# Gated slot attention with a feed-forward layer: both states from one product with e^s stationary, and the low-rank products of two chunks at once

## The reference

```
q, k = rope(x Wq^T), rope(x Wk^T);  v, g = x Wv^T, x Wg^T
s  = clip(x Ws1^T Ws2^T + bs2, -32, 32)        # low rank: 16
z  = cumlogsumexp(s, over rows);  es = exp(s);  enz = exp(-z)
ok = enz * (tril(q k^T / sqrt(128)) es);  qv = softmax(ok, over the 64 slots)
o  = tril((qv * enz) es^T) v
o  = o * rsqrt(mean(o^2) + 1e-5) * g_norm * (g * sigmoid(g))
x1 = layernorm(x + o Wo^T);  out = layernorm(x1 + x1 (W * scale)^T + bias)
```

## Time and profile before

| | us |
|---|---|
| median of 3 runs | 1460.3 (1459.96 to 1460.4) |
| the profiled execution | 1457.91 |
| its span | 1456.1 |
| busy: PE, PEld | 1426.3, 1204.2 |
| busy: DVE, POOL, ACT | 951.5, 521.1, 491.3 |
| mean granted TensorE clock | 0.996 of full |

### The profile page before, as it was taken

How to read it: one execution, slowest core, us unless ns; L and a number is a source line. 1 busy time by engine, 2 the same in 40 slices (tenths; PEclk the granted TensorE clock), 3 DMA queues, 4 the chain that set the end, 5 groups by cost and what they waited for, 6 DMA issues and landing times.

```text
span 1456.1 us, 23764 instructions
## 1 busy us (share of the span) xinstructions
PE 1426.3 (98%) x9664; PEld 1204.2 (83%) x9664; DVE 951.5 (65%) x1635; ACT 491.3 (34%) x965; POOL 521.1 (36%) x440
## 2 busy tenths in 40 slices
PE   5999999999999999999999999999999999999988
PEld 4888888888888888888888888888888888888876
DVE  5756666566765666567765656657675666657677
ACT  4323223233322323223432322223432222323356
POOL 3322333334433333234533323334432333333255
PEclk9999999999999999999999999999999999999999
DMA  5210111113211201112211110222222021201223
GB/s 203 81 36 33 66 44 59 37 64 120 75 69 44 72 23 55 62 57 97 102 66 30 54 64 26 70 73 67 87 80 66 24 72 44 69 26 66 66 99 118
DMA packets 39562, 97.06 MB, mean 67 GB/s; under 512 B 4384, under 2 KB 4512, under 8 KB 35616
## 3 DMA queue, kind: packets, MB, share of 16 engines
q1 hardware_dynamic: 36864, 90.85, 18.7%
q10 hardware_dynamic: 2592, 4.72, 0.9%
HBM read 74.58 MB, written 20.97 MB: 66 GB/s over the span
## 4 chain that ended last, share of the span: by engine, by line
PE 85%; POOL 7%; DVE 3%; issue 2%; ACT 2%; DMA 0%; POOLq 0%; SPq 0%; ACTq 0%; DVEq 0%
PE bank_kg L941 25%; PE bank_qv L941 13%; PE bank_a L941 12%; PE bank_t L973 6%; POOL o_gated L463 5%; PE bank_wo L1183 4%; PE bank_e L986 3%; PE bank_wo L1159 3%; POOL rms L461 2%; PE bank_a L999 2%; PE bank_qv L958 2%; PE bank_qv L960 2%; PE bank_qv L961 2%; PE bank_c L1188 2%; DVE sum_sq L907 2%
## 5 line engine op out<-in xcount | busy, mean ns | idle before, releaser
L461 POOL TENSOR_TENSOR rms<-var,minus_half 128x4 f32<-128x4 f32 x64 | 65.1, 1017 | 537.3 <-DVE var L910 537.3
L941 PE MATMUL bank_kg<-w_hi,hs_hi 128*128 128x512 f32 x512 | 207.9, 406 | 2.0 <-DVE w_lo L677 1.9
L941 PE MATMUL bank_kg<-w_hi,hs_lo 128*128 128x512 f32 x512 | 202.7, 396 | 0.0
L941 PE MATMUL bank_kg<-w_lo,hs_hi 128*128 128x512 f32 x512 | 201.9, 394 | 0.0
L941 PE MATMUL bank_a<-wo_hi,oT 128*128 128x512 f32 x512 | 174.6, 402 | 0.0
L958 PE MATMUL bank_qv<-hs_hi,w_hi 128*128 128x256 f32 x504 | 146.5, 291 | 9.0 <-DVE w_lo L677 9.0
L758 DVE RECIPROCAL enzT<-cumsT 128x256 f32<-128x256 f32 x64 | 112.2, 1752 | 63.8 <-ACT cumsT L551 51.7
L429 POOL TENSOR_TENSOR k_rot<-rope_a,rope_b 128x512 f32<-128x512 f32 x64 | 82.7, 1292 | 183.4 <-DVE rope_b L706 183.4
L960 PE MATMUL bank_qv<-hs_lo,w_hi 128*128 128x256 f32 x504 | 141.1, 280 | 0.0
L961 PE MATMUL bank_qv<-hs_hi,w_lo 128*128 128x256 f32 x504 | 141.0, 280 | 0.0
L424 POOL TENSOR_TENSOR qT<-rope_a,rope_b 128x512 f32<-128x512 f32 x64 | 82.7, 1292 | 160.7 <-DVE rope_b L718 160.7
(11 more groups left out here) (172 smaller groups left out, 3225.3 us busy)
## 6 DMA issues: line engine op xcount, KB each, us to landing
w_raw<-w_groups SPq DMA_DIRECT2D x28, 1024.0 KB, 5.0
hs_raw<-hs_cols SPq DMA_DIRECT2D x64, 256.0 KB, 2.8
x_scratch<-part SPq DMA_DIRECT2D x64, 256.0 KB, 2.0
part<-x_scratch SPq DMA_DIRECT2D x48, 256.0 KB, 2.8
part<-hs_rows SPq DMA_DIRECT2D x16, 256.0 KB, 3.0
w_raw<-x_scratch SPq DMA_DIRECT2D x16, 256.0 KB, 3.1
w_raw<-w_groups SPq DMA_DIRECT2D x14, 256.0 KB, 6.1
out<-gate ACTq DMA_DIRECT2D x8, 256.0 KB, 2.1
```

The lines of the kernel that those rows point to most:

```text
L461: pool.tensor_tensor(rms[:, :], var[:, :], minus_half[:, :], ALU.pow).then_inc(rms_made, 1)
L941: mm = pe.matmul(dst, x, y, start=start and n == 0, stop=stop and n == 2, **kw)
```

## The change

The rotated k and v of a head stand side by side in one buffer (`kv`). With es of the head as the stationary operand (64 columns), one product of 256 moving columns then makes both es^T k and es^T v, that is, s1 transposed, and s2. So before s1 can be used, PE turns it back with two transposes into bank_e, at the start of the next chunk, and ScalarE copies it to SBUF; the product of s1 with q moves behind the transposes of o_gated. The low-rank products of the loop take two chunks at once, in every second chunk, from the split inputs with a split Ws1: eight float32r matmuls of 256 moving columns, four with 128 stationary columns and four with 64. They stand right behind the q projection. The load of an input chunk no longer waits for the low-rank product. The twelve small tiles for each row slot's norm factors become one tile with twelve columns (not shown).

```diff
-        u_rounded, u_scaled = sb("u_rounded", P, F32R), sb("u_scaled", P)
+
+        ws1_split = sb("ws1_split", KT * P, F32R)
+        u_rounded, u_scaled = sb("u_rounded", 2 * P, F32R), sb("u_scaled", 2 * P)
...
+        kv = [sb(f"kv{s}", 2 * F)[:, :] for s in range(2)]
...
-        s1, s2 = states[:, 0:H], states[:, H:2 * H]
+        pT, states, s1 = sb("pT", H), sb("states", 2 * H), sb("s1", H)
...
-        s1_acc, s2_acc = bank_c[:, 0:H], bank_c[:, H:2 * H]
+        s1_acc = bank_e[:, 0:H]
...
+        def has_low_rank(i):
+
+            return i % 2 == 1 and i + 3 <= CHUNKS
...
+        def kv_of(slot, which):
+            return kv[slot].rearrange("p (h e x) -> p h e x", e=2, x=P)[:, :, which, :]
...
                     sp.wait_ge(hs_lo_made, i + 2)
-                    if i + 2 <= CHUNKS:
-                        sp.wait_ge(u_mm, i + 2)
                     load_hs(c % 2, (i + 3) % CHUNKS)
...
-                pool.tensor_tensor(k_rot[slot][:, :], rope_a[:, :], rope_b[:, :], ALU.add).then_inc(k_summed, 1)
+                pool.tensor_tensor(kv_of(slot, 0), per_head(rope_a[:, :]), per_head(rope_b[:, :]), ALU.add).then_inc(k_summed, 1)
...
-            def u_hi(n):
+            def u_hi(n, chunks=1):
 
                 act.wait_ge(u_mm, n)
-                if n > 1:
-                    act.wait_ge(u_made, n - 1)
-                act.activation(u_rounded[:, :], u_acc, ACT.Identity, bias=one_row).then_inc(u_hi_made, 1)
-                copy(u_scaled[:, :], u_acc, u_of_own).then_inc(u_hi_made, 1)
+                if n > chunks:
+                    act.wait_ge(u_made, n - chunks)
+                cols = slice(0, P * chunks)
+                act.activation(u_rounded[:, cols], u_acc[:, cols], ACT.Identity, bias=one_row
+                               ).then_inc(u_hi_made, chunks)
+                copy(u_scaled[:, cols], u_acc[:, cols], u_of_own).then_inc(u_hi_made, chunks)
...
+            copy(ws1_of(0), ws1_tiles()).then_inc(ws1_hi_made, 1)
...
+                if c:
+                    from_bank(s1[:, :], s1_acc, s1_mm, carried(u, c - 1), s1_made)
                 if not left:
                     tick(1, 1)
+                if has_low_rank(i):
+                    u_hi(i + 3, 2)
                 if i > 1:
                     from_bank(oT_hi, bank_t[:, :], oT_mm, i - 1, oT_hi_made)
                 if not left:
                     tick(2, 2)
-                if i + 2 <= CHUNKS:
-                    u_hi(i + 2)
...
+                if has_low_rank(i):
+                    u_lo(i + 3, 2)
...
+            def s2_of(h):
+                at = 2 * P * (h // 2) + P
+                return states[64 * (h % 2):64 * (h % 2) + 64, at:at + P]
...
+            def low_rank_pair(n):
+
+
+                pair, _ = half_of(n)
+                for k in range(KT):
+                    hi, lo = cols((hs_hi[pair % 2], hs_lo[pair % 2]), 2 * P * k, 2 * P)
+                    pe.matmul(u_acc, ws1_split[:, P * k:P * k + P], hi, start=k == 0, stop=False,
+                              skip_group_check=True)
+                    mm = pe.matmul(u_acc[0:64, :], ws1_split[:, P * k:P * k + 64], lo, start=False,
+                                   stop=k == KT - 1, skip_group_check=True)
+                mm.then_inc(u_mm, 2)
...
@@ -1079,29 +1118,39 @@
                     for k in range(KT):
                         mm = project_q(i + 2, bank_qv, k)
                     mm.then_inc(q_mm, 1)
+                if has_low_rank(i):
+                    pe.wait_ge(ws1_lo_made, 1)
+                    if i > 1:
+                        pe.wait_ge(o_gated_made, i - 1)
+                    low_rank_pair(i + 2)
 
                 if not left:
                     pe.wait_ge(states_made, carried(u, c - 1))
                     turn_x1(0, 0)
-                pe.wait_ge(a_masked, i)
                 if c:
                     pe.wait_ge(states_made, carried(u, c - 1))
+                    pe.wait_ge(cumsT_made, 2 * i)
+                    for r in range(2):
+                        mm = pe.transpose(s1_acc[:, P * r:P * r + P], states[:, 2 * P * r:2 * P * r + P], ident)
+                    mm.then_inc(s1_mm, 1)
+                pe.wait_ge(a_masked, i)
 
                 for h in range(HG):
                     head = slice(P * h, P * h + P)
                     mm = pe.matmul(okT_of(h), es[now][:, M * h:M * h + M], masked[:, head], start=h < 2,
                                    stop=c == 0, skip_group_check=True)
+                if not c:
+                    mm.then_inc(okT_mm, 1)
+
+                if i > 1:
+                    pe.wait_ge(o_norm_made, i - 1)
+                    transposes(o_gated).then_inc(oT_mm, 1)
                 if c:
+                    pe.wait_ge(s1_made, carried(u, c - 1))
                     for h in range(HG):
                         mm = pe.matmul(okT_of(h), s1[:, M * h:M * h + M], qT_of(i, h), start=False, stop=True,
                                        skip_group_check=True)
-                mm.then_inc(okT_mm, 1)
-
-                if i > 1:
-                    pe.wait_ge(o_norm_made, i - 1)
-                    transposes(o_gated).then_inc(oT_mm, 1)
-                if i + 2 <= CHUNKS:
-                    low_rank(now)
+                    mm.then_inc(okT_mm, 1)
...
-                if i + 2 <= CHUNKS:
-                    pe.wait_ge(u_hi_made, 2 * (i + 2))
+                if has_low_rank(i):
+                    pe.wait_ge(u_hi_made, 2 * (i + 3))
...
-                        mm = pe.matmul(o_of(h), pT[rows, at], s2[rows, at], start=False, stop=False,
+                        mm = pe.matmul(o_of(h), pT[rows, at], s2_of(h), start=False, stop=False,
...
-                    transposes(k_rot[nxt]).then_inc(kT_mm, 1)
+                    transposes(kv[nxt], apart=2 * P).then_inc(kT_mm, 1)
...
-                    mm = pe.matmul(o_of(h), masked[:, head], v[now][:, head], start=False, stop=True,
+                    mm = pe.matmul(o_of(h), masked[:, head], kv[now][:, 2 * P * h + P:2 * P * h + 2 * P], start=False, stop=True,
                                    skip_group_check=True)
                 mm.then_inc(o_mm, 1)
                 if c < CB - 1:
+
+
                     for h in range(HG):
-                        pe.matmul(s1_acc[:, M * h:M * h + M], k_rot[now][:, P * h:P * h + P],
-                                  es[now][:, M * h:M * h + M], start=c == 0 and h == 0, stop=True,
-                                  skip_group_check=True)
-                    for h in range(HG):
-                        rows, at = slice(64 * (h % 2), 64 * (h % 2) + 64), slice(DV * (h // 2), DV * (h // 2) + DV)
-                        mm = pe.matmul(s2_acc[rows, at], es[now][:, M * h:M * h + M], v[now][:, DV * h:DV * h + DV],
-                                       start=False, stop=True, skip_group_check=True)
+                        mm = pe.matmul(bank_c[64 * (h % 2):64 * (h % 2) + 64, 2 * P * (h // 2):2 * P * (h // 2) + 2 * P],
+                                       es[now][:, M * h:M * h + M], kv[now][:, 2 * P * h:2 * P * h + 2 * P],
+                                       start=c == 0 and h < 2, stop=True, skip_group_check=True)
                     mm.then_inc(states_mm, 1)
```

More of the change, by code:

```diff
@@ L84, in gated_slot_attention_block @@
         scale_row = sb("scale_row", D)
-        u_rounded, u_scaled = sb("u_rounded", P, F32R), sb("u_scaled", P)
+        ws1_split = sb("ws1_split", KT * P, F32R)
+        u_rounded, u_scaled = sb("u_rounded", 2 * P, F32R), sb("u_scaled", 2 * P)
         u_all = sb("u_all", CHUNKS * P, F32R)
         masked, o_sq, kT = [sb(n, F)[:, :] for n in ("masked", "o_sq", "kT")]
-        v, gate = [[sb(f"{n}{s}", F)[:, :] for s in range(2)] for n in ("v", "gate")]
+        gate = [sb(f"gate{s}", F)[:, :] for s in range(2)]
+        kv = [sb(f"kv{s}", 2 * F)[:, :] for s in range(2)]
         prob, okT, s_clip = [sb(n, H)[:, :] for n in ("prob", "okT", "s_clip")]
@@ L98, in gated_slot_attention_block @@
         rope_a, rope_b = sb("rope_a", F), sb("rope_b", F)
-        k_rot = [sb(f"k_rot{s}", F) for s in range(2)]
         es_hi = [sb(f"es_hi{s}", H, F32R) for s in range(2)]
@@ L131, in gated_slot_attention_block @@
         ok_acc = bank_wo[:, 512:512 + H]
-        u_acc = bank_wo[:, 512:512 + P]
+        u_acc = bank_wo[:, 512:512 + 2 * P]
         def w2_of(h):
@@ L166, in gated_slot_attention_block @@
         for name in ("first", "second"):
-            norms.append([[sb(f"{name}_{what}{s}", n) for s in range(LAST)] for what, n in
-                          (("stats", 6), ("mean_var", 2), ("var_eps", 1), ("neg_mean", 1), ("rstd", 1), ("shift", 1))])
+            four = [sb(f"{name}_norm{s}", 12) for s in range(LAST)]
+            norms.append([[t[:, a:z] for t in four] for a, z in ((0, 6), (6, 8), (8, 9), (9, 10), (10, 11), (11, 12))])
         const_in, ws1_in, ws2_in, scale_in = sem("const_in"), sem("ws1_in"), sem("ws2_in"), sem("scale_in")
@@ L186, in gated_slot_attention_block @@
```

(24 more changed lines are left out.)

12 lines of the change are left out of this document (5 added, 7 removed).

## The result

The changed kernel takes 1466.2 us (median of 7, 1464.2 to 1466.4) against 1460.2 (median of 7, 1458.8 to 1460.9): ratio 1.004, 95% interval 1.0029 to 1.005. The forecast was 1465.8, with a range from 1457 to 1475. The profiled execution's span is 1463.0 us, 6.9 above that of before.

A forecast was written before the change was run, and what follows sets the result against it. PE's own instruction stream was taken to set the time. Terms -22.1 + 10.6 + 17.3 + 3.8 - 4.1 = +5.5 us gave 1463.4 for the profiled execution and 1465.8 for the median, range 1457 to 1475.

The forecast's parts named there:

- The bound: Whole kernel: PE's own instruction stream sets the time, so a change is worth its effect on distances between PE's starts.
- step 4: Second-chunk o_gated transposes: PE's wait for GpSimd grows from 0.17 to about 0.41 us, +3.8 us over 16.
- Step 1: State stage, 48 chunks: s1's passes go, s2's matmuls widen to 256 columns; net -0.46 us a chunk, -22.1 us.
- Step 2: Two transposes turning s1 back before okT, 48 chunks: +0.22 us each, +10.6 us, with ScalarE's copy covered.
- step 3: s1 product behind the o_gated transposes, 48 chunks: changes of array form in and out cost 0.36 us each, +17.3 us.
- step 5: Low-rank products: fourteen leave the loop, -10.4 us; seven f32r pairs come in, +6.6; filled waits -0.35; sum -4.1 us.
- Step 6: The rest (k and v writes, ScalarE's u copies, input loads, prologue): put at nothing.
- (a): Low-rank pair: array forms alternate inside it, +6.9 us on the sum, 1472.7 us; chance 25%.
- (b): Wide state passes: bound by weight loads, not by the stream; whole 3 us faster; chance 8%.
- (d): Wide state passes: two don't run side by side, +41 us, 1507 us; chance 3%.
- (c): s1 product's way in overlaps with the o_gated transposes and the wait doesn't grow: -8 and -3.8 us, 1454; chance 15%.

The follow-up runs named there:

- e10: Changed kernel with the state product of all four heads in one half of the columns, in second and third chunks: 1490.8 us, ratio 1.0214.
- e11: Changed kernel with the state product moving only the 128 columns of v, the k part left out, in second and third chunks: 1451.4 us, ratio 0.9944.
- e5: Changed kernel with the four heads of the state product in the order 0, 2, 1, 3: 1465.9 us, ratio 1.0045.
- e3: Changed kernel with the two s1 transposes inside the q projection and the s1 product back behind okT: 1445.2 us, ratio 0.9902.
- e9: e3 with the s1 transposes moved behind the q projection, where the changed kernel has them: 1449.1 us, ratio 0.9931.
- e2: Kernel before the change with one edit, the s1 product moved behind the transposes of o_gated: 1478.0 us, ratio 1.0131.
- e4: Changed kernel with VectorE's wo_lo moved from the end of the first chunk to the second chunk, behind oT_lo: 1458.4 us, ratio 0.9995.
- e1: Kernel before the change with all of the low-rank edits and none of the others: 1455.2 us, ratio 0.9973.
- e6: Changed kernel with 128 stationary columns instead of 64 in the four low matmuls of the low-rank pair: 1466.6 us, ratio 1.0042.
- e7: e3 with VectorE's wo_lo moved as in e4: 1446.6 us, ratio 0.991.

## Why the prediction was right, step by step

**The bound** was right in the main: nearly every figure above adds up from PE's starts alone. Other engines mattered in the second chunks, as step 4 says, and at two places that it does not name: in the three fourth chunks in front of a change of weights, where VectorE's weight split is just in time (about 0.5 us of the forecast cost is hidden there), and in the last sequence.

**Step 1** was forecast at -0.46 a chunk and is -0.41 (timeline and table above): the middle value, two concurrent streams of 0.8 ns a column, is shown by e10 and e11. The mis-sized term is the late second pair, 0.05 us that the wider first pair does not hide. 48 x 0.05 = 2.4 us too favourable. The theory of e5 read it as needing neighbours in different halves; the runs show that the order doesn't matter, which left the number untouched.

**Step 2**, +0.22, holds: e3 keeps the transposes and its fourth chunks, which have no state stage, are 0.22 slower than before. The copy is covered as said; e9 measures the chain at 0.75 us against the 0.8 used. What the cover is worth was not worked out before the order was chosen: with okT alone as cover, the copy costs 0.12 a chunk (e9), a third of what step 3 pays to hide it.

**Step 3** was put at +0.36 and is 0.32 to 0.35 (fourth chunks 0.54 - 0.22; e2 0.35): 48 x 0.03 = about 1.5 us too dear. Taking the price from the old low-rank product, in the same place and form, gave it before any run. The ten early chunks that had paid for the forms with their low-rank product make no exception in the changed kernel: there the old product's 0.77, counted in step 5, goes as a whole. e2 keeps that product, and there they cost nothing. A reading in this step is 0.1 off: from the last q matmul (707.29) to VectorE's okT (709.80) it is 2.5 us, not 2.4. The conclusion holds: in the changed kernel VectorE takes up okT at 710.99, as soon as its work on q is done.

**Step 4**: 0.17 was to grow to about 0.41, measured 0.37, so +0.2 and not +0.24 a second chunk; e4 shows the cause by taking it away, 0.40 a chunk. Two chunks of the last sequence wait 1.2 and 0.9 us for o_gated (before, 0.4 and nothing); VectorE and GpSimd also have the first norms to do there, but no run takes them away. That wasn't forecast. One costs 0.65 in the loop, the other is in the 0.7 behind it.

**Step 5** was -4.1 and e1 has -4.1 in the loop. Going by the data type and not by the written form was the choice that mattered; e6 bears it out. The remark of the Trainium skill, PSUM — Partial Sum Buffer, section The four PSUM rules, on float32r and the column group mask is in line with the 0.12 us spacing. Its mark in the forecast, "all 128\*128", was wrong: the trace writes 128\*64, and only the distance of starts tells.

**Step 6** holds within what the profile resolves.

**Rivals.** (a) falls by e1 and e6, (b) by e11, (d) by e10's contrast. (c) falls in both parts by e2. One sum of the prediction doesn't come out: 8 x 0.24 = 1.9 us a pair, seven times, would have made (a) about 1479, above the range; its 1472.7 goes with about 1.0 a pair, that is, eight changes of 0.12. Since (a) falls, nothing else hangs on it.

**Luck.** Of its own terms the forecast had step 1 2.4 us too good and steps 3 and 4 some 1.5 and 0.6 too dear, the weight changes hide 0.5 and the last sequence adds 0.65. So the mechanism was right, and part of the closeness of 0.4 us is that errors of 1 to 2 us cancel.

## What to carry to other kernels

Where PE is never idle, price an edit by distances between starts of its instructions, and count the changes of array form that an order makes: here each way in or out costs 0.09 to 0.16 us, and 0.05 more come before the second pair. Price the wait that an order is to hide as well: 0.33 us to hide a 0.75 us copy is more than waiting for it behind okT (0.12). A copy between two products of PE is hidden best inside a long run of one form, as the q projection, where small work of the same form costs only its own time (0.22 us for two transposes, e3). When a stage gets shorter, look at what was just in time before: a wait of 0.17 us, too short for the list of waits, grew to 0.37, by half of the 0.41 that the stage saved. The same goes for a cure: moving wo_lo took the wait away in e4 and made another in e7.

## What the runs showed of the hardware that was not expected

- Matmuls of 64 stationary columns in different halves of the columns run at once even when two of one half are issued in a row (e5, 1465.9 us against 1466.2); in one half they take 1.87 us instead of 1.01 (e10). So in these kernels a pass did not wait for passes of the other half that were issued ahead of it.
- The form 128\*64 at an f32r matmul is no change of form: 0.12 us between starts (e1 and the changed kernel), the same as with 128 columns (e6).
- GpSimd's tensor_tensor that starts 0.64 us after a 2.34 us VectorE instruction takes 2.60 us instead of 1.04 and ends 0.90 after it (after, 748.33); started 0.22 after, 3.02 and 0.90. With VectorE's instruction elsewhere, it takes 1.04 each time (e4). The es_lo of e7, 0.75 by itself, starts with a VectorE instruction of 2.28 us, takes 2.85 and ends 0.58 after it. In all three cases what is left after VectorE's end is GpSimd's own time less 0.14 to 0.17 us. It looks as if it makes almost no headway until VectorE's instruction is over; which VectorE instructions do this was not tested.
- The stretch in front of the first scores differs by up to 2.5 us between profiled executions of kernels that don't differ there: 36.5 us in e11, 37.2 in the changed kernel, 39.0 in e6. The granted clock differs with it. From 20 to 25, 25 to 30 and 30 to 35 us it was 0.93, 0.73 and 1.00 in e11, 1.00, 0.66 and 1.00 in the changed kernel, and 0.97, 0.50 (the lower level, 1.2 GHz) and 0.85 in e6. That the clock is the cause is not shown.
